# Modulation rows in PSUM, kernel exponentials first, and GpSimd's side work reordered in a one-core adaLN block

## The reference, cut to what matters

```python
mod = (silu(c) @ wmod).reshape(4, 6, 1, 128)          # c: 4 x 128, wmod: 128 x 768
sa, ca, ga, sb, cb, gb = (mod[:, m] for m in range(6))
ga, gb = (sign(g) * maximum(abs(g), 0.25) for g in (ga, gb))      # sign(0) = 1
h  = layernorm(x) * (1 + ca) + sa                      # x: 4 x 1024 x 128
xn = layernorm(h) * ln_g + ln_b
x_proj, z = split(xn @ in_w.T + in_b)                  # 2 x 128 columns
log_A = clip(-exp(A_log) * clip(exp(log_dt)))          # 128 channels x 16 states
kernel[l, d] = sum_n exp(l * log_A[d, n]) * C[d, n] * B[d, n] * dt[d]
y = causal_conv(x_proj, kernel) * silu(z)
x = x + ga * clip(y @ out_w.T + out_b + h, -10, 10)
h = layernorm(x) * (1 + cb) + sb
t = h @ W_proj + b_proj;  e = argmax(t @ W_gate)       # top-1 of 8 experts
o = gelu(layernorm(t @ W1[e] + b1[e])) @ W2[e] + b2[e]
out = x + gb * layernorm(o)
```

## Time and profile before

| | us |
|---|---|
| median of 3 runs | 322.46 |
| lowest, highest | 320.94, 323.23 |
| the profiled execution, own time | 319.81 |
| its span in the trace | 317.1 |
| busy in it: PE, DVE, ACT, POOL | 265.2, 241.1, 147.8, 173.5 |

### The profile page before, as it was taken

How to read it: one execution, slowest core, us unless ns; L and a number is a source line. 1 busy time by engine, 2 the same in 40 slices (tenths; PEclk the granted TensorE clock), 3 DMA queues, 4 the chain that set the end, 5 groups by cost and what they waited for, 6 DMA issues and landing times.

```text
span 317.1 us, 6528 instructions
## 1 busy us (share of the span) xinstructions
PE 265.2 (84%) x1755; PEld 169.3 (53%) x1756; DVE 241.1 (76%) x932; ACT 147.8 (47%) x371; POOL 173.5 (55%) x194
## 2 busy tenths in 40 slices
PE   0888777996899699859868999999999999999740
PEld 0543434575896377546333456565655655656430
DVE  1899999899984999986990677777777767778730
ACT  3394765863432358732010454645545445455420
POOL 2745776700000255440046758888888888887561
PEclk9999999999999959955989999999999999999985
DMA  6830005999706989835103222232232222221000
GB/s 149 204 132 1 1 2 100 292 263 269 182 4 238 291 224 286 236 102 167 53 2 84 90 65 86 65 91 71 68 95 63 80 83 66 86 76 45 17 14 0
DMA packets 47145, 35.22 MB, mean 111 GB/s; under 512 B 4546, under 2 KB 42421, under 8 KB 46994
## 3 DMA queue, kind: packets, MB, share of 16 engines
q1 hardware_dynamic: 42434, 24.64, 28.8%
q0 software_dynamic: 3744, 9.77, 10.7%
q10 hardware_dynamic: 944, 0.53, 0.7%
HBM read 24.27 MB, written 11.08 MB: 112 GB/s over the span
## 4 chain that ended last, share of the span: by engine, by line
DVE 29%; POOL 27%; issue 23%; PE 15%; DMA 2%; POOLq 1%; DVEq 1%; ACT 1%; SPq 1%; ACTq 0%
POOL SBk L566 13%; POOL rs L584 9%; POOL out_dram L574 4%; DVE st L798 4%; DVE Hh L831 3%; PE PS L1305 2%; PE PS L1281 2%; DVE Hh L843 2%; DVE SBk L369 2%; DVE mv L805 2%; DMA CP<-in_L_attn_C_param_dram 2%; PE PS L1250 2%; DVE PS L983 2%; DVE PS L985 2%; PE PS L1205 2%
## 5 line engine op out<-in xcount | busy, mean ns | idle before, releaser
L747 ACT ACTIVATE V<-PS,gb1T 128x128 f32<-128x128 f32 x156 | 58.7, 457 | 59.5 <-PE PS L1445 58.1
L484 POOL TENSOR_TENSOR rs<-ve,half 128x4 f32<-128x4 f32 x24 | 24.4, 1018 | 74.9 <-DVE ve L809 72.5
L1454 PE MATMUL PS<-BIG,V 128*128 x312 | 47.4, 292 | 3.4 <-DVE Wst L1163 1.8
L566 POOL DMA_INDIRECT SBk<-rows,idgi x39 | 41.8, 1071 | 12.8 <-issue 7.6
L1454 PEld LDWEIGHTS PS<-BIG,V 128*128 128x128 f32 x312 | 43.5, 196 | 6.3 <-issue 4.5
L574 POOL DMA_INDIRECT out_dram<-Wst,idsi x39 | 39.7, 1017 | 11.1 <-issue 11.1
L1157 DVE TENSOR_SCALAR V<-PS,mv,rs 128x512 f32<-128x512 f32 x39 | 31.4, 806 | 17.0 <-POOL rs L584 16.7
L1437 PE MATMUL PS<-BIG,V 128*128 x78 | 40.6, 602 | 1.6 <-issue 1.6
L584 POOL TENSOR_TENSOR rs<-ve,half 128x2 f32<-128x2 f32 x42 | 30.6, 730 | 11.5 <-DVE ve L1178 10.6
L1147 DVE BATCH_NORM_STATS2 st<-PS 128x6 f32<-128x512 f32 x39 | 27.0, 693 | 8.7 <-PE PS L1439 8.3
L1445 PE MATMUL PS<-ident,V 128*128 128x128 f32 x156 | 25.6, 287 | 0.0
(11 more groups left out here) (243 smaller groups left out, 519.5 us busy)
## 6 DMA issues: line engine op xcount, KB each, us to landing
BIG<-k_pad SPq DMA_DIRECT2D x32, 256.0 KB, 5.6
X<-in_L_attn_x_dram SPq DMA_DIRECT2D x4, 512.0 KB, 7.3
BIG<-in_L_ffn_W_dram SPq DMA_DIRECT2D x1, 2048.0 KB, 9.2
rows<-GL SPq DMA_DIRECT2D x4, 512.0 KB, 5.3
rows<-Hh SPq DMA_DIRECT2D x8, 256.0 KB, 3.7
out_dram<-Hh SPq DMA_DIRECT2D x8, 256.0 KB, 3.9
rows<-U SPq DMA_DIRECT2D x4, 512.0 KB, 3.2
Wst<-la_rows SPq DMA_DIRECT2D x1, 1024.0 KB, 4.7
```

Of the source, the lines that this page charges most:

```text
L566: pool.indirect_dma_start(out=XG[:, u, :], out_offset=None, in_=rows, in_offset=bass.IndirectOffsetOnAxis(ap=idgi[:, t:t + 1], axis=0), bo ...
L747: a.activation(AT[:, u, k, :], PS[:, 3, P * k:P * k + P], ACT.Gelu, bias=gb1T[:, 1, bass.ds(e, 1), k], scale=gb1T[:, 0, bass.ds(e, 1), k]) ...
L1454: m.matmul(dst, AT[:, u, k, :], W2s[:, bass.ds(e, 1), k, :].rearrange("p a d -> p (a d)"), start=(k == 0), stop=False)
```

## The change

- The rows sa and ca stay in PSUM banks 6 and 7 (`MODP`), and both groups of `modulate` read them there; the 1 is added to ca by a product of ones on TensorE. `MOD` keeps the two gates only, copied later.
- silu(c) is made as c / (1 + exp(-c)) with VectorE's help, and ScalarE's 16 exponentials of `KN` stand in front of its copies of weights.
- ScalarE makes `inwG`; in_b is added in PSUM; GpSimd makes the three bf16 parts.
- GpSimd: the kernel factors and the bias parts go first, the kernel sums around the first two units, then one piece of `V` after each of units 2 to 5, then the memsets.
- `modulate`: means and variances of h of the unit before stand at its head, `nb` stands in front of the second group.
- Loads: six small ones ahead of x of batch rows 1 to 3, three more by ScalarE's queue; raw weights load into `YS` instead of `NR`.
- TensorE: 6 fill products instead of 11 ahead of the units; the one in each unit stands behind the wait for the unit's banks.

```diff
@@ sync: loads
                 for dst, src in ((BP[:], B_param), (CP[:], C_param)):
                     sp.dma_start(dst, src).then_inc(s_bcp, 16)
-                for b in range(1, B):
-                    sp.dma_start(X[:, b], x[b].rearrange("(i p) d -> p i d", p=P)).then_inc(s_x, 16)
                 for dst, src in ((outw, out_w), (wpr[:], W_proj), (wgt[:], W_gate),
...
                     sp.dma_start(dst, src).then_inc(s_w, 16)
+                for b in range(1, B):
+                    sp.dma_start(X[:, b], x[b].rearrange("(i p) d -> p i d", p=P)).then_inc(s_x, 16)
@@ gpsimd
-            def norm_step(q, h, clear):
+            def norm_step(q, h):
...
+            def in_bias_parts():
+                pool.wait_ge(s_rc, 1)
+                pool.wait_ge(s_bel, 1)
+                for m in range(2):
+                    step.mark(g.tensor_copy(part_in[:], row_in[:]))
+                    step.settle()
+                    step.mark(g.tensor_tensor(row_low[:], part_in[:], bc(below[:, m:m + 1], [3, 2 * D]), ALU.mult))
+                    step.settle()
+                    step.mark(g.tensor_tensor(row_in[:], row_in[:], row_low[:], ALU.add))
+                    step.settle()
+                g.tensor_copy(part_in[:], row_in[:]).then_inc(s_r1e, 1)
...
+            rstd(0, 0, s_vx, s_rx, 1)
+            pool.wait_ge(s_cb, 1)
+            pool.wait_ge(s_ke, 1)
+            kernel_factors(0)
+            rstd(0, 1, s_vx, s_rx, 2)
+            kernel_factors(1)
+            in_bias_parts()
+            kernel_sum(8)
+            norm_step(1, 1)
+            for n in (4, 2):
+                kernel_sum(n)
+            step.settle()
+            g.tensor_tensor(KP[:, 0:P], KN[:, 0], KN[:, 1], ALU.add).then_inc(s_kp, 1)
+            for q in range(2, 2 * B - 1):
+                norm_step(q, q % 2)
+                if q < 6:
+                    v_exponents(q - 2)
                 else:
-                    zero_states(q - 5)
...
+                    zero_states(0)
             pool.wait_ge(s_n, 5)
             rstd(1, 0, s_vh, s_rh, 2 * B - 1)
-            zero_states(2)
+            zero_states(1)
             pool.wait_ge(s_n, 6)
             rstd(1, 1, s_vh, s_rh, 2 * B)
+            zero_states(2)
             zero_states(3)
@@ scalar
-            a.activation(scT[:], cT[:], ACT.Silu).then_inc(s_silu, 1)
...
+            a.activation(ecT[:], cT[:], ACT.Exp, scale=-1.0).then_inc(s_ec, 1)
...
+            a.copy(inwT[:], PS[:, 0, 0:2 * D]).then_inc(s_iwc, 1)
+            a.activation(inwG[:], PS[:, 0, 0:2 * D], ACT.Copy, scale=lngc[:, 0:1]).then_inc(s_inw, 1)
...
             act.wait_ge(s_lb, 16)
...
+            act.wait_ge(s_gp, 1)
+            for m in range(2):
+                last = a.copy(MOD[:, m].rearrange("p b d -> p (b d)"), PS[:, 2 + m, :])
+            last.then_inc(s_me, 1)
@@ vector: modulate
-                before = step.now()
+                if not first:
+                    step.settle()
+                    step.mark(row_means(1, o))
+                    step.settle()
+                    row_vars(1, o).then_inc(s_vh, 1)
                 if not last:
                     sums_x = step.mark(row_stats(tiles(X, b + h, o), 0, o))
-                if not first:
-                    step.settle(before)
-                    means_h = step.mark(row_means(1, o))
-                if first:
-                    dve.wait_ge(s_me, 1)
                 src, dst = tiles(X, b, h), tiles(Hh, b, h)
-                ca1, sa = (MOD[:, bass.ds(b, 1), m, :].rearrange("p a d -> p (a d)") for m in (1, 0))
+                ca1, sa = mod_row(b, 1), mod_row(b, 0)
...
                 scaled = step.mark(ins)
-                if not first:
-                    step.settle(means_h)
-                    row_vars(1, o).then_inc(s_vh, 1)
                 if not last:
                     step.settle(sums_x)
                     means_x = step.mark(row_means(0, o))
+                if not first:
+                    dve.wait_ge(s_rh, q)
+                    shifts(o).then_inc(s_nb, 1)
                 dve.wait_ge(s_rx, q + 1)
...
                 if not last:
                     step.settle(means_x)
                     row_vars(0, o).then_inc(s_vx, 1)
-                if not first:
-                    dve.wait_ge(s_rh, q)
-                    shifts(o).then_inc(s_nb, 1)
                 step.settle(shifted)
                 step.mark(row_stats(dst, 1, h))
@@ tensor
             for b in range(B):
...
+                m.matmul(MODP[:, b].rearrange("p m d -> p (m d)"), bc(scT[:, b:b + 1], [P, P]), wmf[:, 0:2 * D],
+                         start=True, stop=False, skip_group_check=True)
+                m.matmul(MODP[:, b, 1, :], ones3[0:1, :], ones3[0:1, :], start=False, stop=True,
+                         skip_group_check=True).then_inc(s_mod, 1)
```

More of the change, by code:

```diff
@@ L602, in _ @@
             act.wait_ge(s_c, 16)
-            a.activation(scT[:], cT[:], ACT.Silu).then_inc(s_silu, 1)
-            for b in range(B):
-                act.wait_ge(s_mod, b + 1)
-                for m, one in ((0, 0.0), (1, 1.0), (2, 0.0)):
-                    last = a.activation(MOD[:, b, m, :], PS[:, 2 + b, m * D:m * D + D], ACT.Copy, bias=one)
-                last.then_inc(s_me, 1)
-            act.wait_ge(s_ptr, 1)
-            a.copy(inwT[:], PS[:, 0, 0:2 * D])
-            a.copy(outwT[:], PS[:, 0, 2 * D:3 * D])
-            a.copy(wprT, PS[:, 0, 3 * D:4 * D]).then_inc(s_etr, 1)
+            a.activation(ecT[:], cT[:], ACT.Exp, scale=-1.0).then_inc(s_ec, 1)
             act.wait_ge(s_la, 2)
@@ L779, in _ @@
             v.tensor_scalar(LA32[:, 0:NS], EA[:], LOG_LO, 0.0, ALU.max, ALU.min).then_inc(s_la, 1)
+            dve.wait_ge(s_iota, 1)
+            for m in range(2):
+                last = v.tensor_scalar(below[:, m:m + 1], part[0:3], m + 0.5, -1.0, ALU.is_ge, ALU.mult)
+            last.then_inc(s_bel, 1)
+            dve.wait_ge(s_la, 1)
+            v.transpose(LAT[:], LA32[:]).then_inc(s_la, 1)
+            dve.wait_ge(s_ec, 1)
+            step.mark(v.tensor_scalar(ecT[:], ecT[:], 1.0, None, ALU.add))
+            step.settle()
+            step.mark(v.reciprocal(ecT[:], ecT[:]))
+            step.settle()
+            v.tensor_tensor(scT[:], cT[:], ecT[:], ALU.mult).then_inc(s_silu, 1)
             dve.wait_ge(s_bcp, 32)
@@ L866, in _ @@
             step.mark(row_stats(tiles(X, 0, 0), 0, 0))
-            for m in range(2):
-                v.tensor_scalar(below[:, m:m + 1], part[0:3], m + 0.5, -1.0, ALU.is_ge, ALU.mult)
             step.settle()
@@ new lines, in _ @@
+                m.matmul(MODP[:, b, 1, :], ones3[0:1, :], ones3[0:1, :], start=False, stop=True,
+                         skip_group_check=True).then_inc(s_mod, 1)
+            pe.wait_ge(s_w0, 16)
+            m.transpose(PS[:, 0, 0:D], inw[:, 0, :], ident[:])
+            m.transpose(PS[:, 0, D:2 * D], inw[:, 1, :], ident[:]).then_inc(s_iwt, 1)
+            for k, col in enumerate((2, 5)):
+                for b in range(B):
+                    last = m.matmul(PS[:, 2 + k, b * D:b * D + D], bc(scT[:, b:b + 1], [P, P]), wm[:, col, :],
+                                    start=True, stop=True)
```

167 lines of the change are left out of this document (84 added, 83 removed).

## The result

| | before | after |
|---|---|---|
| median, us | 321.70 (4 runs) | 326.23 (4 runs) |
| lowest, highest | 319.71, 323.23 | 325.82, 327.58 |
| profiled execution, its span | 319.81, 317.1 | 327.58, 325.8 |

The ratio is 1.0164, 95% interval 1.0125 to 1.0203: slower by 1.6%. I had forecast 331.8 with a range of 322.5 to 335.5, as 9.3 us on top of a median of 322.46; the medians here are 4.5 us apart.

The account below looks back on a forecast made before the run. The prediction took the normalisation of x and h, up to VectorE's eighth `nb`, as the bound: 9.1 + 1.2 - 1.0 = +9.3 us on a median of 322.46 gave 331.8 us, range 322.5 to 335.5.

Parts of the forecast that it names:

- rival B: In the loop, VectorE's `ve` of h comes before GpSimd's V product and is not held: 324.5 us, chance 0.20.
- Third to sixth shifts: Loop units: GpSimd's V product holds `ve` of h 1.63 us; 6.95 us a unit against 5.36 to 5.8, sixth `nb` 60.5.
- Modulation rows in PSUM: VectorE's modulate groups: PSUM operands escape GpSimd's holds but cost 0.06 us per instruction, 1.24 against 1.0 a group.
- +9.1: Forecast delay in us of the eighth `nb` on VectorE: 69.4 against 60.34 before.
- GpSimd's queue to the first shifts: Start: GpSimd's factors, bias parts (4.9 us) and sum precede `rstd` of h; first `nb` at 26.3 against 27.31.
- Second shifts: Second unit: GpSimd's sum of four rows holds `ve` of h until 30.1; second `nb` at 32.7 against 32.67.
- Seventh and eighth: Last two units: a memset replaces V, units of 4.8 and 4.1 us, `nb` at 65.3 and 69.4.
- Behind it: After the eighth `nb`: two memsets hold VectorE's SBUF copies about 1.9 us, against 0.6 before: +1.2 us.
- -1.0 from the Toeplitz blocks: States' stage: kernel in DRAM some 15 us earlier, Toeplitz blocks ready, TensorE no longer late: -1.0 us.
- The sum: Whole kernel: 9.1 + 1.2 - 1.0 = +9.3 us, added to a median of 322.46.
- Rival D: TensorE: the forecast plus a lower granted clock behind an idle stretch of some 3 us, 3.4 to 4 us more; chance 0.14.
- Rival C: The change delivers: PSUM operands free, bias parts 2 us on GpSimd, second unit not held; 318.1 us, chance 0.13.

Follow-up runs that it names:

- e1: The changed kernel with the order inside `modulate` of the kernel before, rows still in PSUM: 314.51 us, ratio 0.9847 to the kernel before.
- e2: The changed kernel without GpSimd's four V products (V filled with -1 at the start): 319.9 us, ratio 1.0016 to the kernel before.
- e6: The changed kernel with GpSimd's V products halved and put between the two `rstd` of a unit: 321.94 us, ratio 1.0017 to the kernel before.
- e3: The kernel before with only the new order inside `modulate`, rows in SBUF: 324.48 us, ratio 1.0137 to the kernel before.
- e4: e1 with the modulation rows copied to SBUF by ScalarE and read there: 319.78 us, ratio 1.0018 to the kernel before.
- e9: e5 with eight small unused matmuls more on TensorE, ahead of the units: 316.25 us in one run.
- e8: e5 with `rstd` of h ahead of the bias parts on GpSimd and other side work spread over units: 315.05 us, ratio 0.9825 to the kernel before.
- e10: e8 with the last eight table transfers issued later: 311.14 us, ratio 0.9705 to the kernel before.
- e11: e5 with the last eight table transfers issued later: 314.60 us, ratio 0.9802 to the kernel before.
- e7: The changed kernel, its order kept, with the modulation rows copied to SBUF by ScalarE: 329.20 us, ratio 1.0258 to the kernel before.
- e5: e1 with all four memsets moved to GpSimd's idle time at the start: 314.73 us, ratio 0.9820 to the kernel before.

## Why the prediction was right, and where its sizes were off

The direction, the place and the mechanism were right; the forecast was 5.6 us too high, and the measured time lies inside its range. The range is wide and takes in rival B, whose 324.5 lies nearer to 326.23 than my 331.8: it is the trace, not the time, that decides for the forecast's mechanism.

- **Third to sixth shifts.** The deciding term. `ve` of h came 0.22 us behind GpSimd (0.27 worked out) and was held 1.70 us (1.63), in four units. Rival B needed it to come first; it never did. e1, e2 and e6 each take away the meeting in another way, and each time the hold is gone and the time falls; e3 brings the meeting into the kernel before, and its time rises.
- **Modulation rows in PSUM: the term that was mis-sized.** I took 0.06 us more for each instruction from the L971 of the earlier trace rows, 1.24 for a group. L882 and L894 take 1.10 and 1.11 with the last one's tail, as L831 does in the earlier trace rows: zero, the lower bound. It makes 2.4 us of the 3.1 between +9.1 and the +6.0 that the eighth `nb` shows: 0.47 in each of the four long units, 0.24 in each of the last two. The rest is in the way from the end of the hold to L882 (0.71 us from 37.22, and not 1.23), since the means of h stand ahead of the hold now; the means of x, which I had left out of that sum, take half of it back ahead of `nb`. A unit is 6.24 instead of 6.95. The neighbour was a tensor_tensor that writes over its own input and waits for TensorE group by group, not the same instruction. e4 shows what the rows bring: they escape the hold (1.09 us for the four L881 of e1, 2.02 for the four L886 of e4). In the order of after that hold falls on `ve`, where the rows cannot help.
- **GpSimd's queue to the first shifts.** 26.3 forecast, 26.55 measured, but two errors cancel here, which is luck. I had the modulation rows ready at 11.1, "just when VectorE asks", by scaling the 384 columns of before down to 256. They took 1.36 us for each batch row and not 0.97, ended at 12.76, and VectorE stood idle 1.42 us before 12.81; so the second half of the factors ended at 19.05 and not 17.9. The parts took 4.25 us, not 4.9 (inside the bounds), and the sum 2.33. **Second shifts:** 32.7, and 32.73.
- **Seventh and eighth.** Units of 4.44 and 3.92 against 4.8 and 4.1; mostly the same PSUM term.
- **Behind it.** From the eighth `nb` to the state scan before took 60.34 to 76.77, 16.43 us; after, 66.34 to 83.72, 17.38: +0.95 for the held copies (+1.2).
- **-1.0 from the Toeplitz blocks: the size right at first, the reason wrong.** TensorE gains 0.92 on the states (+6.03 at L1349 against +6.95 at the scan). But in the kernel before it waits for no transfer in that stage. What makes it late there are the same idle stretches that e9 puts down to a place in its code, 128 records apart:

```profile
75.87 1.39 PE L1295 MATMUL PS<-U,Wst 128*32 128x32 f32 x66 [2.64 <-issue]
...
80.15 3.08 PE L1281 MATMUL PS<-BIG,U 128*32 128x128 f32 x101 [1.20 <-issue]
```

Now they are 0.59 and 3.42 us, together as long as before (4.01 and 3.84). TensorE is no longer late because it starts the stage 4.92 us later (73.49 against 68.57) and the states come 6.95 later. The gain is given back: the products that follow the states' stage start at 103.81 against 97.00, +6.8, since TensorE waits 0.88 us for the first states and 0.73 in the same stage for `YS`.
- **The sum.** +6.8 by the end of the first stage in the traces; the medians differ by 4.5, and of my 5.6 us too much 0.8 are the median of before, 321.70 where I started from 322.46. The profiled execution of before lies 1.9 under its median and that of after 1.4 over; some 2 us of the first stage's 6.8 do not show in the medians, and which executions lack them the traces cannot tell.
- **Rival D, the clock.** It was the forecast, and on top of it a lower granted clock behind an idle stretch of some 3 us, as in the earlier trace rows (3.09 us, then 0.66), for 3.4 to 4 us; with it the range reaches up to 335.5. No run shows those 3.4 to 4 us: the price of a lower clock at the same place is 1.2 us in e8 (granted 0.58 and 0.57) and 1.7 in e1 (0.50 from 76 to 78). In the changed kernel the idle stretch came (3.42 us), but the clock stayed at 1.00 from 84 to 97; behind shorter stretches of 2.05 and 2.06 us it fell in e6 and e1, so length alone does not decide. Nor is the stretch idle time for the states: it stands at the place in the code that e9 moved.
- **Rival C** took PSUM at nothing, rightly; but it took the parts at 2 us (4.25) and the second unit as not held, and that was held 1.06 at 29.34.

## What to carry over

When VectorE and GpSimd share work, write down for each small tensor_scalar, copy or scalar_tensor_tensor of VectorE that reads SBUF only which long GpSimd instruction starts just ahead of it: 0.2 us of lead cost 1.5 us a unit, and moving and halving the product gave that back with the same work. Operands in PSUM are the other way out, and cost nothing in scalar_tensor_tensor here (1.10 us for four L882, 1.10 for four L831 with both rows in SBUF). And where TensorE runs short instructions back to back, keep bulk transfers off that stretch and off the few us ahead of it: with eight transfers issued later TensorE's stop falls from 3.70 to 0.41 us, and e10 is 1.2% faster than e8.

## What the runs showed that I had not expected

- TensorE stopped at places in its code that lie 128 matmul records and 128 weight loads apart: for 1.2 to 3.7 us where bulk transfers ran at the time or just before (before, the second stretch of after, e8, and the first of e10), and for 0.4 us where they had been over for 3 us (second stretches of e10 and e11). The kernel before has these stops too (2.64 and 1.20 us). Such a stretch, marked "issue" by the profile, is no wait of the program.
- After such a stop of 3.70 us in e8 the granted clock was 0.57 for 4 us, after one of 2.06 in e1 it was 0.50 from 76 to 78, and in e6 and e7 (2.05 and 3.15 us; 0.50 from 78 to 81 and from 87 to 90) the same 106 records took 4.89 and 4.88 us; after 3.42 us in the changed kernel, 2.86 in e2, 2.31 in e5 and 1.76 in e4 they took 3.22, at 1.00. What decides the clock stays open.
- GpSimd's memset holds a copy of VectorE (1.70 instead of 0.16) but not `nb`, which reads two tensors and started 0.09 us behind the same memset at 66.34, at 0.16. In the kernel before, four scalar_tensor_tensor with all rows in SBUF took 1.11 us from 55.12, beside a memset from 54.96; four of the same form beside a product took 2.02 (e4).
- The power of a 128x4 tile on GpSimd, 1.01 us long, does not hold a scalar_tensor_tensor: in e4 it runs from 37.39, and the four L898 with rows in SBUF take 1.10 from 37.46.
- A product does not hold the statistics: in the kernel before three of them take 0.66 us from 39.11, beside GpSimd's sum from 39.17, as they do elsewhere.
